# Alternating a unit's short TensorE matmuls with the slot's long ones

## What is computed

```
xn = layernorm(x)
q = rope(xn @ wq)   # 32 heads of 128
k = rope(xn @ wk)   #  8 heads of 128
v = xn @ wv         #  8 heads of 128
scores = q . k * 128**-0.5     # per head, 256 x 256
allowed = (j <= i) & (j > i - 128)
attn = softmax(where(allowed, scores, -max))
out = (attn . v) @ wo
x = x + out
```

## Time and profile before

| | |
|---|---|
| median of three runs | 727.85 us |
| the profiled execution | 728.14 us |
| its span in the trace | 726.4 us |
| TensorE matmul busy, share of the span | 98% |
| TensorE weight loads busy | 83% |
| VectorE, ScalarE, GpSimd busy | 72%, 58%, 55% |
| granted TensorE clock | full, in all 40 slices |
| DMA | mean 45 GB/s, 32.34 MB |

### The profile page before, as it was taken

How to read it: one execution, slowest core, us unless ns; L and a number is a source line. 1 busy time by engine, 2 the same in 40 slices (tenths; PEclk the granted TensorE clock), 3 DMA queues, 4 the chain that set the end, 5 groups by cost and what they waited for, 6 DMA issues and landing times.

```text
span 726.4 us, 13750 instructions
## 1 busy us (share of the span) xinstructions
PE 714.5 (98%) x3699; PEld 603.5 (83%) x3699; DVE 522.3 (72%) x1773; ACT 424.3 (58%) x1146; POOL 396.5 (55%) x515
## 2 busy tenths in 40 slices
PE   8999989999999999999999999999999999999998
PEld 6887768888888888888888888888888888887886
DVE  6778776767777777677776677676767776778784
ACT  3456675556664675557655766476657665655440
POOL 2365676535853496447743765368535864374630
PEclk9999999999999999999999999999999999999999
DMA  8140013000310022002100120003000310030002
GB/s 274 56 166 29 0 39 93 15 0 8 100 40 2 0 77 68 1 1 73 58 15 1 58 73 15 1 28 103 15 2 0 102 29 0 1 117 1 0 31 88
DMA packets 25870, 32.34 MB, mean 45 GB/s; under 512 B 5834, under 2 KB 14282, under 8 KB 25300
## 3 DMA queue, kind: packets, MB, share of 16 engines
q1 hardware_dynamic: 25232, 30.69, 13.4%
q10 hardware_dynamic: 580, 1.05, 0.4%
HBM read 27.55 MB, written 4.19 MB: 44 GB/s over the span
## 4 chain that ended last, share of the span: by engine, by line
PE 88%; DVE 4%; POOL 4%; ACT 1%; issue 1%; DMA 1%; SPq 0%; DVEq 0%; POOLq 0%; ACTq 0%
PE bank L1192 33%; PE bank L1253 24%; PE bank L1235 8%; PE bank L1214 7%; PE bank L1153 4%; PE bank L1222 4%; PE bank L1211 2%; POOL wo_lo L405 1%; PE bank L1175 1%; PE bank L1201 1%; PE bank L1212 1%; DVE stats L789 1%; PE bank L1138 1%; PE bank L1126 1%; PE bank L1143 1%
## 5 line engine op out<-in xcount | busy, mean ns | idle before, releaser
L413 POOL TENSOR_TENSOR swap<-swap,rope 128x512 f32<-128x512 f32 x80 | 104.5, 1307 | 116.3 <-ACT swap L593 115.8
L420 POOL TENSOR_SCALAR_AFFINE_SELECT pT_hi_lo<-pT_hi_lo 128x256 fp32r<-128x256 f32 x128 | 52.4, 409 | 140.4 <-DVE pT_hi_lo L943 140.4
L619 ACT ACTIVATE bank<-sm,nmax 128x128 f32<-128x128 f32 x128 | 47.6, 372 | 105.1 <-DVE nmax L928 105.0
L627 ACT ACTIVATE pT_hi_lo<-bank 128x256 fp32r<-128x256 f32 x128 | 49.2, 385 | 95.1 <-PE bank L1222 62.8
L593 ACT ACTIVATE swap<-bank 64x512 f32<-64x512 f32 x160 | 95.1, 594 | 15.0 <-PE bank L1192 12.5
L943 DVE TENSOR_TENSOR pT_hi_lo<-bank,pT_hi_lo 128x256 fp32r<-128x256 f32 x128 | 53.8, 420 | 52.5 <-ACT pT_hi_lo L627 52.2
L430 POOL TENSOR_TENSOR q_lo<-rot,q_hi 128x512 fp32r<-128x512 f32 x64 | 82.7, 1293 | 1.3 <-ACT q_hi L601 1.3
L1253 PE MATMUL bank<-wo_hi,oT_hi 128*128 128x512 f32 x256 | 74.6, 413 | 0.0
L1192 PE MATMUL bank<-xnT_lo,wq_hi 128*128 128x512 f32 x256 | 73.3, 389 | 0.0
L894 DVE TENSOR_TENSOR rot<-bank,rope 128x512 f32<-128x512 f32 x80 | 55.1, 689 | 25.2 <-ACT swap L593 25.1
L1192 PE MATMUL bank<-xnT_hi,wq_hi 128*128 128x512 f32 x256 | 71.9, 393 | 1.0 <-DVE v_lo L914 0.8
(11 more groups left out here) (158 smaller groups left out, 1695.2 us busy)
## 6 DMA issues: line engine op xcount, KB each, us to landing
raw<-in_L_attn_wq SPq DMA_DIRECT2D x32, 256.0 KB, 2.9
raw<-in_L_attn_wo SPq DMA_DIRECT2D x32, 256.0 KB, 2.7
x<-in_L_attn_x SPq DMA_DIRECT2D x4, 512.0 KB, 7.4
raw<-in_L_attn_wk SPq DMA_DIRECT2D x8, 256.0 KB, 2.6
raw<-in_L_attn_wv SPq DMA_DIRECT2D x8, 256.0 KB, 2.6
out<-x SPq DMA_DIRECT2D x8, 256.0 KB, 2.0
raw<-in_L_ffn_W_base ACTq DMA_DIRECT2D x4, 256.0 KB, 5.3
wb_keep_hi<-q_hi SPq DMA_DIRECT2D x1, 1024.0 KB, 4.9
```

Source lines behind the costliest of these rows:

```text
L413: nc.gpsimd.tensor_tensor(w, w, tab, ALU.mult).then_inc(t2_done, 1)
L420: nc.gpsimd.affine_select(pT_both[:, :, 2, h, :], pT_both[:, :, 1, h, :].bitcast(F32), pattern=[[0, 2], [1, P]], compare_op=ALU.is_ge, fil ...
```

## The change

The five pieces of `scores` and the two of `p_transpose` are handed out one at a time. Behind each score piece stands one long matmul of the slot: of `values` or `out_project` where the slot has a tail, and in slots 0 and 4, which have none, one of up to 4 (slot 0) or 2 (slot 4) projections held back from the slot's nine. Behind the first transpose stands one more of the tail, and behind the second the tail's rest. The number of matmuls, their operands and their sizes stay as they were, and so do the waits, each at the first or the same piece of its function as before. The first sequence's slots and the last half's projections are not held back. The other engines' programs are not touched.

```diff
+def between(s, n, plain):
+    return min(n, 2 if s == 4 else 4) if s % G == 0 and not plain else 0
...
-            def scores(u, s, j, hf):
+            def scores(u, s, j, hf, step_):
...
-            def values(beta, par, b, j):
+            def values(beta, par, b, j, lo=0, hi=9):
...
-            def out_project(beta, par, i, g):
+            def out_project(beta, par, i, g, lo=0, hi=12):
...
-                        project(target(g, last, hf), 1 if last else 1 - hf, pos[s], pos[s + 1], g if last else g + hf)
+                        held = between(s, pos[s + 1] - pos[s], start or last and hf == 1)
+                        dst = target(g, last, hf), 1 if last else 1 - hf
+                        gw = g if last else g + hf
+                        project(*dst, pos[s], pos[s + 1] - held, gw)
...
-                        if s < SLOTS - 1:
-                            scores(u + 1, s + 1, j, hf)
-                        elif not (last and hf == 1):
-                            scores(u + 1, 0, j + 1, 1 - hf)
-                        if not (start and s == 0):
-                            p_transpose(u - 1, s - 1)
+                        def tail(lo, hi):
+                            if s % G == 1 and not start:
+                                values(beta - 1, prev_hf, (b - 1) % 2, j - (s < G), lo, min(hi, 9))
+                            if s % G >= 2 and not start:
+                                out_project(beta - 1, (b - 1) % 2, s % G - 2, g if b else g - 1, lo, hi)
+
+                        nxt = (u + 1, s + 1, j, hf) if s < SLOTS - 1 else None if last and hf == 1 else (u + 1, 0, j + 1, 1 - hf)
+                        for piece in range(5):
+                            if nxt:
+                                scores(*nxt, piece)
+                            if piece < held:
+                                project(*dst, pos[s + 1] - held + piece, pos[s + 1] - held + piece + 1, gw)
+                            tail(piece, piece + 1)
+                        for c in range(2):
+                            if not (start and s == 0):
+                                p_transpose(u - 1, s - 1, c)
+                            if c == 0:
+                                tail(5, 6)
...
-                        if s % G == 1 and not start:
-                            values(beta - 1, prev_hf, (b - 1) % 2, j - (s < G))
-                        if s % G >= 2 and not start:
-                            out_project(beta - 1, (b - 1) % 2, s % G - 2, g if b else g - 1)
+                        tail(6, 12)
```

More of the change, by code:

```diff
@@ L1202, in v_transpose @@
                 last.then_inc(vt_done, 1)
-            def scores(u, s, j, hf):
+            def scores(u, s, j, hf, step_):
                 b, h = s // G, s % G
-                pe.wait_ge(qlo_done, 5 * j + 2 + h)
-                wait(pe, norm_done, u - 1)
                 q0, q1 = (slice(b * SEQ + i * P, b * SEQ + (i + 1) * P) for i in range(2))
-                mm(S[s % 2][:, 0:2 * P], q[0][:, hf, h, q0], k_both[:, :, hf, q0], start=True, stop=False)
-                mm(S[s % 2][:, 0:P], q[1][:, hf, h, q0], k[0][:, hf, q0], start=False, stop=True)
-                for n, (a, c) in enumerate(PASSES):
+                if step_ == 0:
+                    pe.wait_ge(qlo_done, 5 * j + 2 + h)
+                    wait(pe, norm_done, u - 1)
+                    mm(S[s % 2][:, 0:2 * P], q[0][:, hf, h, q0], k_both[:, :, hf, q0], start=True, stop=False)
+                elif step_ == 1:
+                    mm(S[s % 2][:, 0:P], q[1][:, hf, h, q0], k[0][:, hf, q0], start=False, stop=True)
+                else:
+                    n = step_ - 2
+                    a, c = PASSES[n]
@@ L1214, in scores @@
                     last = mm(S[s % 2][:, 2 * P:4 * P], q[a][:, hf, h, q1], k[c][:, hf, b * SEQ:(b + 1) * SEQ],
                               start=(n == 0), stop=(n == 2))
[L1216 to L1223, removed]
@@ L1239, in out_project @@
-            def out_project(beta, par, i, g):
[L1241 to L1248, removed]
+                    if n == 2:
+                        last.then_inc(s_done, 1)
@@ new lines, in p_transpose @@
+            def p_transpose(u, s, c):
+                if c == 0:
+                    pe.wait_ge(norm_done, u + 1)
+                    wait(pe, ptlo_done, u)
+                last = tp(T[:, c * P:(c + 1) * P], prob[:, s % 2, c * P:(c + 1) * P], ident[:, :])
+                if c == 1:
+                    last.then_inc(t_done, 1)
+            def values(beta, par, b, j, lo=0, hi=9):
+                for step_ in range(lo, hi):
+                    if step_ == 0:
+                        pe.wait_ge(a_free, 6 * j + 6)
+                        pe.wait_ge(ptlo_done, 4 * beta + 4)
+                        wait(pe, otlo_done, 2 * beta)
+                    if step_ == 6:
+                        pe.wait_ge(parted, 4 * beta + 4)
+                    i = 0 if step_ < 3 else 1
+                    blk, kb = ((0, 0), (1, 0), (2, 1))[step_ // 3]
+                    a, c = PASSES[step_ % 3]
+                    last = mm(O[i][:, :], v[a][:, par, 2 * b + kb, :], pT[c][:, blk, :, :],
+                              start=(step_ in (0, 3)), stop=(step_ in (2, 8)))
+                    if step_ in (2, 8):
+                        last.then_inc(pv_done, 1)
@@ new lines, in out_project @@
+            def out_project(beta, par, i, g, lo=0, hi=12):
+                for step_ in range(lo, hi):
+                    a, c = PASSES[step_ // G]
+                    h = step_ % G
+                    if step_ == 0:
+                        pe.wait_ge(conv_hi, wo_pos(g, G - 1) + 1)
+                        pe.wait_ge(othi_done, 2 * beta + i + 1)
+                        if wo_bank(beta, i) is C:
+                            wait(pe, x_added, 2 * beta + i)
+                        else:
+                            pe.wait_ge(otlo_done, 2 * beta + 2)
+                    if h == 0 and c:
@@ L1249, in out_project @@
                         pe.wait_ge(conv_lo, wo_lo(g, G - 1))
-                    if a:
+                    if h == 0 and a:
                         pe.wait_ge(otlo_done, 2 * beta + i + 1)
[L1252 to L1255, removed]
+                    last = mm(wo_bank(beta, i)[:, :], oT[a][:, par, i, h, :], wo_s[c][:, h, :],
+                              start=(step_ == 0), stop=(step_ == 11))
@@ L1257, in group @@
+                    if step_ == 11:
+                        last.then_inc(c_done, 1)
             def group(g, first, last):
@@ L1342, in _ @@
             project(0, 0, 36, 72, 0)
-            scores(0, 0, 0, 0)
+            for piece in range(5):
+                scores(0, 0, 0, 0, piece)
             group(0, True, False)
@@ L1347, in _ @@
             group(KV - 1, False, True)
-            p_transpose(16 * KV - 1, SLOTS - 1)
+            for c in range(2):
+                p_transpose(16 * KV - 1, SLOTS - 1, c)
             lora_router(1, 0)
```

1 line of the change is left out of this document (added).

## The result

The changed kernel takes 741.15 us (median of 4 runs, 740.96 to 741.40) against 727.93 us before; the ratio is 1.0182, interval 1.0164 to 1.0200. That is 13.2 us, outside the predicted range, with the sign that had a chance of 0.27.

What follows compares the result with a forecast made beforehand. TensorE, 98% busy, was taken as bound by its work and pace. Terms -0.5 + 0 + 0.45 - 0.3 = -0.4 us gave 727.7 us on the profiled 728.14, 727.4 against the median; range 724.5 to 731.6.

Steps and rivals of the forecast that it cites:

- (1): Short matmuls set apart among long ones: three loads per slot stay exposed, 58 ns each, as before; gain 0.
- Rival A: Loads hide behind long matmuls: 58 ns vanish at each of 305 lone 128-column matmuls, 17.7 us gain, 709.7 us; chance 0.13.
- (2): Pace of the seven short matmuls: 0.805 us isolated against 0.81 in the block, 6 ns less in 92 slots, 0.5 us gain.
- (3): Slow start of long matmuls behind the block: taken as unchanged, 0; bounds from 0.9 us gain to 3.5 us loss.
- Rival B: Each of 730 lone short matmuls slows the long one behind it: 3.5 us loss, 731.4 us, values' slot 2.90; chance 0.22.
- (4): Waits asked for earlier, by values, out_project in slots 2 and 3, and slot 0's scores: 0.6 to 4.6 us spare, all hidden.
- (5): Tail slots' results come later: last score 0.91 us, second transpose 1.36, slot 3's p_hi 0.9; no TensorE wait, 0.
- (6): Existing waits: two for wo_lo reached 0.23 us earlier each, 0.45 us loss; one for P's low part, 0.29 us gain.
- Rival C: VectorE or ScalarE fall behind after later transposes, beyond slot 2's 0.6 us, in 31 sequences; 0.2 us excess gives 734; chance 0.07.

Runs made afterwards that it cites:

- micro_sizes: TensorE alone, no layer computed: pairs of a 512-column matmul and one of n columns (64 to 448), then rows of n alone; 0.340 to 0.438 us a pair.

## Why the prediction was wrong

- **(1), no gain from hiding loads: right.** The long matmul behind a lone 128-column one still waits 0.06 us for its weights, and with TensorE alone a pair of 512 and 128 columns takes 0.339 us, 0.227 for the one and 0.112, a load, for the other. Rival A, 17.7 us of gain, didn't come in any part.
- **(2), 6 ns less per slot: wrong in sign.** No order tried was faster than the block.
- **(3), the slow start: mis-sized.** Taken as 0; the slots are 0.05 us longer, 92 x 0.05 = 4.6 us, above the highest bound of 3.5. The earlier trace rows show slow long matmuls behind a wait and were read as speaking against a price of lone short ones. Rival B's mark, 2.90 us for the slot with values, came out (2.89); its mechanism, 6 ns for each lone short matmul, did not: the cost does not go with their number.
- **(4), waits that come earlier: right in the loop's slots 2 and 3, wrong in the last half.** The 0.96 us to spare for bank C were read in a steady slot, where nine projections lie between two output projections. The last half has none there, and some 0.9 of the 1.66 us that TensorE waits for x_add come of asking earlier. The slacks were also read where nothing was late yet: `values`, given 1.1 us to spare, stands 0.1 us for p_lo in the first half of five of the loop's groups (p_lo ends at 237.99, the matmul starts at 238.13 and the next 0.33 us later instead of 0.23).
- **(5), "So no wait on TensorE comes of it; 0": this step failed, and it is the largest.** The delay of p_hi was worked out right (0.9 us; ScalarE's idle time in front of it shows it), but followed to one reader, the next transpose of P. VectorE's instructions stand in the program's order: behind p_lo come v_diff, whose reader v_transpose has six long matmuls between it and P's second transpose, and x_add, whose reader in the last half comes within one slot. Moving v_diff alone took back 3.9 us, the old order in the last half 2.7, both 6.5. Of these 6.5, some 0.9 belong to (4), 0.1 is pace of the last half, and 0.3 is in the trace of the old kernel with v_diff moved, too; about 5 us are left for (5).
- **(6), 0.45 us for wo_lo:** half of it is there in the first group (0.23 us over the two slots around the wait, pace included), and in the last group more than that. In the two slots of the last group's first half where values waits for a projection bank and the output projection for wo_lo, the starts show 1.1 us, 1.0 above the pace. That one was not tried apart.

The sum: 6.1 (the two repairs' 6.5 less the 0.1 and the 0.3) + 4.6 (pace, by starts) + 1.0 (those two slots, not tried apart) = 11.7 of 13.2 us. Of the 1.5 us left, 0.5 are the waits of `values` and 0.6 are in the first group above its pace. The held projections take 0.6 us by themselves, within the noise, but taking them out of the whole change gave nothing back. Rival C was the right mechanism at the wrong place, slot 2 of every sequence, and had 0.07.

## What to carry to other kernels

When a matmul is spread out or moved back, follow its result through everything that stands behind its consumer in that engine's order, not only to the result's own reader, and do it again in the first and last stages, where slots are shorter than in the steady one. When a wait moves forward, look there, too, for what lay between it and the work it waits for. In none of these runs was an exposed weight load hidden by putting a long matmul behind a short one: the next load began only when the short one did. More columns per load would shorten what is exposed; that was not tried in the layer. Before an order is changed for TensorE's sake, time both orders of one slot on TensorE alone; it takes one short kernel and shows 0.04 us per slot, which a trace of the old order can't.

## What the runs showed of the hardware

A row of matmuls of 64 columns alone takes 0.109 us each, of 128 0.111, of 256 0.120 to 0.122: with one load per matmul none of these rows is faster than 0.109 us. And the granted clock fell though TensorE never paused. In `micro_sizes`, the row of 32 matmuls with 64 columns, then 160, 192 and 224 columns:

```profile
149.82:153.31 3.49, 3.49 (x34) 3.49 (x32) 0.00 (x0) 0.00 (x0) 1.00 0.02 5
153.31:159.47 6.16, 6.16 (x34) 6.16 (x34) 0.00 (x0) 0.00 (x0) 0.57 0.00 0
159.47:165.40 5.93, 5.93 (x34) 5.93 (x33) 0.00 (x0) 0.00 (x0) 0.59 0.00 0
165.40:168.99 3.59, 3.59 (x35) 3.59 (x33) 0.00 (x0) 0.00 (x0) 1.00 0.00 0
```

Behind the short ones the clock stood at its lower level, 1.2 GHz, for most of two rows (0.57 and 0.59 of full in the mean, 10.2 us in all), which ran at 0.193 and 0.185 us a matmul, and was back at 2.4 GHz in the third, at 0.112. TensorE's recorded busy time was full throughout; the layer itself never lost the clock.
